# Four graph-attention layers on one core: the order of turns on five queues, a repeated cycle against a list written in full

## The chip, the core and the metric

One Trainium2 chip, of which the kernel uses one core. The metric is the device time of one execution in microseconds (us): the median of the runs, from the first instruction to the last and what lies around them. Before the change it is 2925.74 us (3 runs, 2920.73 to 2927.1).

## What is computed

The input is 32 graphs (batches) of 512 nodes with 256 features each, and one 512 x 512 adjacency matrix for all. Four pre-normalised graph-attention layers follow each other, and each adds its result to x:

```python
h = jnp.maximum(_layernorm(x, axis=-1), 0.0)
x = x + _L0_gnn_ref(h, adj, ...)   # 4 heads of 64, masked softmax over neighbours, elu
h = jnp.maximum(_layernorm(x, axis=-1), 0.0)
x = x + _L1_gnn_ref(h, adj, ...)   # mlp 256->512, full attention (no mask), mlp 512->256, masked attention
h = jnp.maximum(_layernorm(x, axis=-1), 0.0)
x = x + _L2_gnn_ref(h, adj, ...)   # masked attention with self edges, elu
h = jnp.maximum(_layernorm(x, axis=-1), 0.0)
x = x + _L3_gnn_ref(h, adj, ...)   # masked attention, relu
```

In each attention e[i,j] = leaky_relu(s_i + t_j), the softmax runs over j, and the result is attention @ (h @ W). The batches do not depend on each other.

## The kernel before

Each batch is a chain of about 100 pieces of matrix work (TensorE, PE), with 150 pieces on VectorE (DVE), 136 on ScalarE (ACT), 4 on GpSimd (POOL) and 2 on SyncE (SP) between them. Five Python generators write them (`tensor_batch`, `vector_batch`, `scalar_batch`, `pool_batch`, `sync_batch`), and every `yield` ends one piece, a *turn*. Before each instruction stand the semaphore waits for what it reads and for the buffer it overwrites. Every queue runs in the order in which its instructions were written.

Three batches are in flight at a time, in three *lanes* (batch modulo 3). A lane has its own R, Z, hT, hw and rowt tiles, whose names end in the lane's number, and its own ring of PSUM banks: banks 0 to 2, banks 3 to 5, and for lane 2 banks 6 and 7 alone (`RINGS`). The tiles O1, oT, HA and junk exist once, so that only one batch at a time can be in the wide part of layer 1.

What sets the order of the turns is the table `TURNS` with the function `in_turns`: for each queue a string for the beginning, a *cycle* that is repeated for every batch, and a string for the end. A digit d in the cycle means: one turn of batch t - d. A `w` is a turn of the weight loading (splitting the weights into a high and a low part, turning the masks).

The names used below, with the lines of the profile:

- PE: L515 all three-part matmuls (`mm3`: high x high, high x low, low x high); L536 transposes of the normalised rows; L560 the transpose TM of the column maxima tm; L572 the transpose "row" of the exponentials E; L584 attention of the layers 1b, 2 and 3 (`attend`); L620 attention of layer 0, one group of 64 instructions for each head; L672 the transposes zT of the tile Z after the full attention; L698 transposes of the residual. The matmuls with `wm2` are the second mlp, 24 of them, and those with `hsr` form S, the column sums.
- DVE: L916 adds zT to O1; L920 and L924 make the low part oTlo; L793 makes the attention weights P in the tile R (four for each row); L846, L848 and L854 give a head's output y0; L857 and L859 add it to x; L767 gives tm; L771 to L777 give A; L930 the low part of the second mlp's output; L806 and L808 hsr; L745 and L742 the variance ve.
- ACT: L1168 makes the high part oThi from O1; L1068 copies projected rows out of PSUM; L1031 and L1022 are the pairs "sx, sq" (`entry_sums`), sum and squares of the x that has been loaded for the batch three later; L1175 and L1177 take the second mlp's output out of PSUM, two of each; L1077 gives E; L1102 and L1104 are a head's exponential and relu; L1083 scales hw; L1045 normalises.
- POOL: L1248 raises ve to the power -1/2 (`power`), with L1250 or L1252 and L1254; L499 makes low parts of weights (`gpsimd_lo`).

In order of the batch, the place that the text speaks of most is this: four zT transposes, each followed by L916 on DVE and L1168 on ACT and a low part on DVE; then 24 `wm2` matmuls in four groups of six, of which each waits for its low part; the last group ends the result in two banks, three matmuls for each. L1175 and L1177 take the two banks out, L930 and L806/L808 follow, and S on PE waits for hsr.

Of the kernel before, what the change touches and what calls it, by code (L numbers as in the profile page):

```python
# [13 lines left out]
B, N, F = 32, 512, 256  # L14
# [52 lines left out]

TURNS = {
    "pe": (
        ("wwww00ww0000000w0ww0ww1ww0www00w1w0111w1ww100ww00001w10000100000011100000000000000120000000012000000"  # L70
         "0000000010101121122121211020211000101020110000001101121111112111020120011010011111020111111100010010"
         "0111111"),
        ("1120011101001010112200112212212021122220221111111121101122110021122121211112021121111122212122111111"),
        ("4453344434333443443553445545545354455555355444444444443455344553544545444445354444444555455454544433"
         "4442233323223232334242334443434243344444433233433333332342433442433434333334243333333444434344333322"
         "3331122212112121223131223233323132323333312222222232211223232132233223322223132223222233323232232211"
         "2220011110001010112020112212212021122220221111211111110122110022110112122110010000111200001111001020"
         "1002212000000000000001111000100000122000000000200010000121111100100001111010110000000111100111000010"
         "01010001011111000"),
    ),  # L80
    "dve": (
        ("wwwwwwwww0000w000000w00w0w000w01w00000w0w000000w00w1000000w1w100w11001101010w01011001000110100000000"
         "010w010100010001100000w00000000000001011111000111101011100002000001000100200001110100212121110202122"
         "2222010220002101111011011001120012120110101112121121112101010111111121112212002201110220002122122001"
         "02011100100"),
        ("2222221122200222111221220110101122010000010202100022221111211121112122102221121101100110110211012211"
         "11111111110100000222111220022001012002021211122122"),
        ("5555554455355534545544553434334344554333435335333554554444534544445545545344455443344443343554454344"
         "4434344444444345353544433555534345333534445455455543434444444244243334434423232333244322222224423322"
         "4434433343333343434244344334223332332323324433432333332233333333224424333424244223232244233344344344"  # L90
         "2332333333313133332222331221212232311112131131132333212222223222313321233232323211122212122221233222"
         "3222212222121211313322231133113121213132223323332312222122222022022121112201010001110221001020021002"
         "2221111211111212210220122111201001110110012112201101101100011020110000001111002110100000200001120202"
         "2100000000000010000000010000100000100000100101101110110011121110201200000120000000000000010202211002"
         "1111001100101011101001000000111001011000110000111011111110000000"),
    ),
    "act": (
        ("wwwwwww0000w00www0w000wwww0wwwwwwww11w11w10ww0w100wwwww1w1w1w1w0000w00w1w20w000020020000000000010000"
         "0000000200000010200001000100000200001111000100100001010021120002012100002110010000111000101010101100"
         "2011010101110010011101021111001011000010011020110101211101101101022202"),  # L100
        ("2022021001220022121122012202220011222120122122112212212221121112211222102211112222112112111110212211"
         "122222211202112121012111211122100002"),
        ("5355353434553355454545345555353344555345455455445545545545454544355554454445445555454544344454545454"
         "5545455445355544443444545445433343545332224424442424343342434424442233444423344343444334344443343334"
         "4344443423334433434334432333433434434343444334244333323343433334422324242312133131331133322333223311"
         "3311223332312332322333333233222222333232233323122233332222323222212333232323333223312322122323222231"
         "2131213312102202002202220121211220222000122210211221221122122222111121122212201212111221212112210111"
         "1102211022211002000011020001100021120212211000100121000000100010000000000001200101011100111100101001"
         "0201110000111101000020020010000000011110000100121001100000110011111010000110110011000011001011011001"
         "010100010110001001111000"),  # L110
    ),
    "pool": (
        ("wwwwwwww0wwwwwwwww10w0w20"),
        ("2202"),
        ("5553444233132201010120"),
    ),
    "sp": (
        ("0"),
        ("32"),
        ("2165544313200"),  # L120
    ),
}
FIRST, ENDS = 3, 4


def in_turns(batch, turns, loading):
    going, loads = {}, loading()

    def go(b):
        if 0 <= b < B:  # L130
            if b not in going:
                going[b] = batch(b)
            next(going[b], None)
# [12 lines left out]
    for left in [loads] + list(going.values()):
        for _ in left:
            pass

# [1199 lines left out]
```

## Time and profile before

| | |
|---|---|
| median of 3 runs | 2925.74 us (2920.73 to 2927.1) |
| the profiled execution | span 2924.5 us from first to last instruction; its own time is not listed apart from the runs', the span is 1.2 us under the median |
| PE busy | 2864.4 us, 98% of the span, 25624 matmuls |
| PE weight loads (PEld) | 2637.4 us, 90% |
| DVE, ACT, POOL busy | 2449.0 us (84%), 2306.6 us (79%), 209.0 us (7%) |
| DMA | 42.06 MB; 2 to 4% of the 16 engines outside the first microseconds |
| granted TensorE clock | mean 0.995 of full speed |

How to read it: "busy" is the union of an engine's instructions. A matmul's end is modelled and overlaps the start of the next, so that PE looks busy up to some 0.15 us after it ran out of work; the distance from start to start tells more. "Idle before" is the engine's idle time ahead of an instruction, "<-" names what ended it. The chain of work is followed back from the last instruction, at each step to what released it.

### The profile page before, as it was taken

Reading aid. Unit: us, or ns where it says so; the run is one execution under the profiler, and the core shown is the slowest. Engines: PE = TensorE matmul, PEld = TensorE weight load, DVE = VectorE, ACT = ScalarE, POOL = GpSimd, SP = SyncE. Lnnn points to the kernel's source line nnn. Section 1 sums busy time; section 2 is a strip of 40 time slices with the busy share of each in tenths; the row PEclk is TensorE's granted clock in tenths of the full one; section 3 lists DMA queues with packets and bytes.
Section 4 is the critical chain, followed back from the end, with each engine's and each line's share of the span. In section 5 each row is a group of like instructions: output and inputs, shape, how many; then the busy total and the mean of one; then the engine's idle time right before and its main releaser. Section 6 shows DMA issues by size and latency. Waiting matters only on the chain.

```text
span 2924.5 us, 66977 instructions
## 1 busy us (share of the span) xinstructions
PE 2864.4 (98%) x25624; PEld 2637.4 (90%) x25624; DVE 2449.0 (84%) x7049; ACT 2306.6 (79%) x6303; POOL 209.0 (7%) x410
## 2 busy tenths in 40 slices
PE   7999999999999999999999999999999999999998
PEld 7899999899999999999999999999999999999886
DVE  6788888888888888888888888888888888888866
ACT  6678778778778787788787788787787877887776
POOL 2000000000000000000000000000000000000000
PEclk9999999999999999999999999999999999999999
DMA  2000000000000000000000000000000000000000
GB/s 80 1 11 14 16 16 16 16 1 16 16 16 16 16 1 16 16 16 16 2 16 16 16 16 16 2 16 16 16 16 13 5 16 16 16 15 2 2 1 30
DMA packets 16799, 42.06 MB, mean 14 GB/s; under 512 B 5344, under 2 KB 7392, under 8 KB 16480
## 3 DMA queue, kind: packets, MB, share of 16 engines
q1 hardware_dynamic: 16480, 37.77, 3.7%
q8 instruction: 205, 3.36, 0.5%
q14 instruction: 114, 0.93, 0.1%
HBM read 20.99 MB, written 16.78 MB: 13 GB/s over the span
## 4 chain that ended last, share of the span: by engine, by line
PE 85%; ACT 9%; DVE 4%; issue 1%; POOL 0%; DMA 0%
PE bank L515 45%; PE bank L584 23%; PE bank L620 7%; PE bank L536 4%; PE bank L572 3%; ACT junk L1022 3%; ACT junk L1031 2%; PE bank L672 1%; DVE O L916 1%; ACT Z L1175 1%; PE bank L560 1%; PE bank L698 1%; ACT Z L1068 1%; DVE oTlo L920 1%; ACT hT2hi L1177 0%
## 5 line engine op out<-in xcount | busy, mean ns | idle before, releaser
L584 PE MATMUL bank<-hw,R 128*128 128x257 f32 x3072 | 707.8, 381 | 1.6 <-ACT hw L1083 1.0
L584 PEld LDWEIGHTS bank<-hw,R 128*128 128x128 f32 x3072 | 567.0, 191 | 74.7 <-issue 3.6
L793 DVE SCALAR_TENSOR_TENSOR R<-bank,E,mask_ne 128x512 f32<-128x512 f32 x640 | 448.9, 741 | 3.1 <-PE bank L572 0.7
L1248 POOL TENSOR_TENSOR rs<-ve,mhalf 128x4 f32<-128x4 f32 x128 | 140.6, 1099 | 2659.4 <-DVE ve L745 1655.8
L1045 ACT ACTIVATE Z<-x,nm,rs 128x256 f32<-128x256 f32 x512 | 276.6, 595 | 52.7 <-DVE x L1010 32.0
L515 PE MATMUL bank<-wfc_hi,oThi 128*128 128x256 f32 (+1 forms) x1024 | 303.3, 296 | 0.0
L515 PE MATMUL bank<-wfc_hi,oTlo 128*128 128x256 f32 (+1 forms) x1024 | 289.8, 283 | 0.0
L515 PE MATMUL bank<-wfc_lo,oThi 128*128 128x256 f32 (+1 forms) x1024 | 289.7, 283 | 0.0
L620 PE MATMUL bank<-hw,R 128*64 128x65 f32 x8192 | 268.3, 224 | 0.3 <-DVE R L793 0.3
L620 PEld LDWEIGHTS bank<-hw,R 128*64 128x64 f32 x8192 | 250.3, 138 | 20.1 <-issue 9.9
L1068 ACT COPY Z<-bank 128x258 f32<-128x258 f32 (+1 forms) x512 | 180.9, 371 | 42.6 <-PE bank L515 41.9
L515 PEld LDWEIGHTS bank<-wfc_hi,oThi 128*128 128x128 f32 x1024 | 193.7, 189 | 4.9 <-DVE hT2lo L815 1.7
L515 PEld LDWEIGHTS bank<-wfc_lo,oThi 128*128 128x128 f32 x1024 | 194.6, 190 | 0.0
L515 PEld LDWEIGHTS bank<-wfc_hi,oTlo 128*128 128x128 f32 x1024 | 194.5, 190 | 0.0
L1077 ACT ACTIVATE E<-A,kshift 128x4 f32<-128x4 f32 (+1 forms) x352 | 83.6, 289 | 127.4 <-DVE A L777 127.3
L1083 ACT ACTIVATE hw<-Z,hw 128x256 f32<-128x256 f32 x384 | 179.8, 503 | 1.2
L1022 ACT ACTIVATE Z<-x,sx 128x256 f32<-128x256 f32 x256 | 129.0, 505 | 44.9 <-DVE x L984 44.6
L515 PE MATMUL bank<-HAhi,oThi 128*128 128x258 f32 x512 | 161.8, 316 | 2.1 <-DVE oTlo L886 2.1
L572 PE MATMUL bank<-identr,E 128*128 128x128 f32 x1024 | 152.8, 276 | 10.4 <-ACT E L1077 10.4
L515 PE MATMUL bank<-HAlo,oThi 128*128 128x258 f32 x512 | 145.4, 284 | 0.0
L515 PE MATMUL bank<-HAhi,oTlo 128*128 128x258 f32 x512 | 144.8, 283 | 0.0
L536 PE MATMUL bank<-identr,Z 128*128 128x128 f32 x1024 | 139.3, 276 | 2.8 <-ACT Z L1045 2.6
(262 smaller groups left out, 8351.0 us busy)
## 6 DMA issues: line engine op xcount, KB each, us to landing
x<-in_x_dram SPq DMA_DIRECT2D x32, 512.0 KB, 3.5
out_dram<-x SPq DMA_DIRECT2D x31, 512.0 KB, 2.6
R<-in_adj_dram SPq DMA_DIRECT2D x2, 512.0 KB, 5.6
Z<-in_L_gnn_mlp_w_dram SPq DMA_DIRECT2D x2, 512.0 KB, 5.4
O<-in_L_gnn_W_fc_dram SPq DMA_DIRECT2D x1, 1024.0 KB, 6.9
out_dram<-x SPq DMA_DIRECT2D x4, 128.0 KB, 2.4
R<-in_L_gnn_W_dram SPq DMA_DIRECT2D x1, 256.0 KB, 3.9
R<-in_L_gnn_W_hand_dram SPq DMA_DIRECT2D x1, 256.0 KB, 6.5
```

Of the source, the lines that this page charges most:

```text
L515: i = e.matmul(out, u, v, start=first and q == 0, stop=last and q == 2, skip_group_check=not group)
L536: i = e.transpose(bk[:, n * 128:(n + 1) * 128], hn[:, n, k * 128:(k + 1) * 128], ident[:, :])
L572: i = e.transpose(bk[:, n * 128:(n + 1) * 128], m["E"][:, 0, h, n:n + 1].broadcast_to([128, 128]), ident[:, :])
L584: ins = e.matmul(bk[:, 0:257], P[:, j, i * 128:(i + 1) * 128], hw[:, j, 0:257], start=(j == 0), stop=(j == NBLK - 1))
L620: ins = e.matmul(bk[c:c + 64, i * 66:i * 66 + 65], P[:, (4 * h + j) % PTILES, i * 128 + c:i * 128 + c + 64], hv[:, j, h, 0:65], start=(j = ...
L793: e.scalar_tensor_tensor(P[:, t, :], bank_of(b, "row", p)[:, :], m["E"][:, 1, h, j:j + 1], mask[:, j, :], ALU.max, ALU.mult).then_inc(up(" ...
L1022: e.activation(hns[b % LANES][:, n, :] if l else junk[:, n, :], xs[b % XSLOTS][:, n, :], ACT.Square, bias=m["sx"][:, n:n + 1], scale=-floa ...
L1045: e.activation(hn[:, n, :], x[:, n, :], ACT.Relu, bias=m["nm"][:, n:n + 1], scale=m["rs"][:, n:n + 1]).then_inc(up("hn", b))
L1068: e.copy(raw[s][:, i, 0:n], bank_of(b, f"h{l}", i)[:, 0:n]).then_inc(up("raw", b))
L1077: e.activation(out, m["A"][:, src, 0:nh, :], ACT.Exp, bias=shift[:, 0:1], scale=sc).then_inc(up("E", b))
L1083: e.activation(hw[:, n, 0:256], raw[s][:, n, 0:256], ACT.Copy, scale=hw[:, n, 256:257]).then_inc(up("hw", b))
L1248: e.tensor_tensor(m["rs"][:, :], m["ve"][:, :], mhalf[:, :], ALU.pow).then_inc(up("rs", b))
```

## The change

Only the order of the turns is another. `TURNS` now holds for each queue one string of all its turns, in which a digit or letter is the batch in base 36 (0 to v); `in_turns` reads it one by one. No instruction is added or removed, and each queue has as many turns as before (PE 3224, DVE 4825, ACT 4394, POOL 147, SP 64). Line numbers below the table are 57 higher than before.

```diff
@@ TURNS @@
     "pe": (
-        ("wwww00ww0000000w0ww0ww1ww0www00w1w0111w1ww100ww00001w10000100000011100000000000000120000000012000000"
...
-        ("1120011101001010112200112212212021122220221111111211101121122110021122121112021121111122212122111111"),
...
+        "w00www0000ww0w0000ww0ww11ww0ww0ww1ww1110ww1ww11w00100001100001100200200122002000000000000200010120000111000100"
...
     "pool": (
-        ("wwwwwwww0wwwwwwwww10w0w20"),
-        ("2202"),
-        ("5553444233132201010120"),
+        "wwwwwwwwwwwwwwwwwww0100021113222433354446555766687779888a999baaacbbbdcccedddfeeegfffhgggihhhjiiikjjjlkkkmlllnm"
+        "mmonnnpoooqppprqqqsrrrtsssutttvuuvuvv"
...
@@ in_turns @@
-    going, loads = {}, loading()
-
-    def go(b):
-        if 0 <= b < B:
-            if b not in going:
-                going[b] = batch(b)
-            next(going[b], None)
-
-    start, cycle, end = turns
-    for c in start:
-        if c == "w":
-            next(loads, None)
-        else:
-            go(int(c))
-    for t in range(FIRST, B - ENDS):
-        for c in cycle:
-            go(t - int(c))
-    for c in end:
-        go(B - 1 - int(c))
-    for left in [loads] + list(going.values()):
+    going, loads = [batch(b) for b in range(B)], loading()
+    for c in turns:
+        next(loads if c == "w" else going[int(c, 36)], None)
+    for left in [loads, *going]:
         for _ in left:
             pass
```

In the middle of the new strings (batches 6 to 21) the order repeats every three batches, where before it repeated every batch. Three places, as the built programs have them:

**ACT at batch 11's second mlp, before.** From the last three L1168 of batch 11 (tile O1) to its first L1175; Z1, x1 are tiles of batch 10's lane, Z2 of batch 11's.

```order
L1168 CAST oThi<-O1 128x512 x3
L1068 COPY Z1<-bank3 128x258
L1068 COPY Z1<-bank4 128x258
L1031 ACTIVATE junk,sx1<-x1 128x256
L1022 ACTIVATE junk,sq1<-x1,sx1 128x256
...
L1175 ACTIVATE Z2<-bank6,b2 128x512
L1177 ACTIVATE hT2hi,hs2<-Z2 128x512
```

The same place after the change (line numbers 57 higher); Z0 is batch 12's head:

```order
L1225 CAST oThi<-O1 128x512 x2
L1125 COPY Z1<-bank3 128x258
L1125 COPY Z1<-bank4 128x258
L1088 ACTIVATE junk,sx1<-x1 128x256
L1079 ACTIVATE junk,sq1<-x1,sx1 128x256
L1225 CAST oThi<-O1 128x512
...
L1225 CAST oThi<-O1 128x512
...
L1159 ACTIVATE Z0<-Z0 128x256
L1161 ACTIVATE Z0<-Z0 128x256
L1232 ACTIVATE Z2<-bank6,b2 128x512
L1234 ACTIVATE hT2hi,hs2<-Z2 128x512
```

Before, all four pairs (L1031, L1022) stand between the last L1168 and L1175. After it, one pair stands ahead of the last L1168 but one, one more ahead of the last, and two behind; batch 12's head pair (L1102 and L1104, now L1159 and L1161) stands ahead of L1175 and no longer behind it.

**DVE at the same place, before.** From the last L916 of batch 11 to batch 10's tm; R0, D0, Z0 are batch 12's.

```order
L916 TENSOR_TENSOR O1<-bank7,O1 128x512
L920 TENSOR_TENSOR oTlo<-O1,oThi 128x512
L857 SCALAR_TENSOR_TENSOR Z0<-Z0 128x256
L859 SCALAR_TENSOR_TENSOR x0<-Z0,x0 128x4x64
L924 TENSOR_TENSOR oTlo<-O1,oThi 128x512
L793 SCALAR_TENSOR_TENSOR R0<-bank2,E0,mask_ne 128x512 x4
L846 TENSOR_SCALAR D0<-bank0 128x4
L848 RECIPROCAL rD0<-D0 128x4
L854 TENSOR_TENSOR Z0<-bank0,rD0 128x256
L745 TENSOR_SCALAR ve1<-sq1 128x4
L767 TENSOR_REDUCE tm1<-Z1 128x1
```

And after the change:

```order
L973 TENSOR_TENSOR O1<-bank7,O1 128x512
L977 TENSOR_TENSOR oTlo<-O1,oThi 128x512
L850 SCALAR_TENSOR_TENSOR R0<-bank2,E0,mask_ne 128x512
L981 TENSOR_TENSOR oTlo<-O1,oThi 128x512
L850 SCALAR_TENSOR_TENSOR R0<-bank2,E0,mask_ne 128x512 x2
L903 TENSOR_SCALAR D0<-bank0 128x4
L905 RECIPROCAL rD0<-D0 128x4
L911 TENSOR_TENSOR Z0<-bank0,rD0 128x256
L802 TENSOR_SCALAR ve1<-sq1 128x4
L824 TENSOR_REDUCE tm1<-Z1 128x1
```

Three P (one of them ahead of the last low part) stand where four stood behind it, and L857, L859 have gone behind tm. On PE the head's group L620 of batch 12 that stood ahead of the zT now stands between the last zT and the `wm2` matmuls.

**POOL at the beginning, before.**

```order
L499 TENSOR_TENSOR wfc_lo<-O,wfc_hi 128x512 x4
L1248 TENSOR_TENSOR rs<-ve,mhalf 128x4
L1250 TENSOR_SCALAR nm<-mv 128x4
L1254 TENSOR_TENSOR nm<-nm,rs 128x4
L1248 TENSOR_TENSOR rs<-ve,mhalf 128x4
L1252 TENSOR_SCALAR nm<-sx 128x4
L1254 TENSOR_TENSOR nm<-nm,rs 128x4
L499 TENSOR_TENSOR wm_lo<-Z,wm_hi 128x256 x4
L499 TENSOR_TENSOR wha_lo<-R,wha_hi 128x256 x2
L499 TENSOR_TENSOR w_lo<-rowt,w_hi 128x256 x2
```

And after the change:

```order
L556 TENSOR_TENSOR wfc_lo<-O,wfc_hi 128x512 x4
L1305 TENSOR_TENSOR rs<-ve,mhalf 128x4
L1309 TENSOR_SCALAR nm<-sx 128x4
L1311 TENSOR_TENSOR nm<-nm,rs 128x4
L556 TENSOR_TENSOR wm_lo<-Z,wm_hi 128x256 x4
L556 TENSOR_TENSOR wha_lo<-R,wha_hi 128x256 x2
L556 TENSOR_TENSOR w_lo<-rowt,w_hi 128x256 x2
L556 TENSOR_TENSOR w_lo<-x,w_hi 128x256 x2
L1305 TENSOR_TENSOR rs<-ve,mhalf 128x4
L1307 TENSOR_SCALAR nm<-mv 128x4
```

The group with L1250 is batch 0's second normalisation, the one with L1252 batch 2's first. Batch 2's and all low parts of weights now stand ahead of batch 0's.

## Rows read from the trace of the kernel before

**Rows 1.** The page's first part: busy time, share of the span, instructions.
```profile
PE 2864.4 (98%) x25624; PEld 2637.4 (90%) x25624; DVE 2449.0 (84%) x7049; ACT 2306.6 (79%) x6303; POOL 209.0 (7%) x410
```

**Rows 2.** Windows: start:end, length, busy us (x), PEclk, DMA share, GB/s.
```profile
1010.58:1277.07 266.49, 264.39 (x2389) 244.19 (x2388) 227.72 (x658) 214.32 (x589) 18.06 (x37) 1.00 0.04 13
```

**Rows 3.** Timeline of POOL: start, us, instruction [idle before <-releaser].
```profile
1010.58 1.20 POOL L1248 TENSOR_TENSOR rs<-ve,mhalf 128x4 f32<-128x4 f32 x1 [32.41 <-DVE ve L742]
...
1277.07 1.20 POOL L1248 TENSOR_TENSOR rs<-ve,mhalf 128x4 f32<-128x4 f32 x1 [32.39 <-DVE ve L742]
```

**Rows 4.** The chain of waits, 1060 to 1150 us: start, us, what.
```profile
1060.01 1.73 PE bank L584 x8
1061.75 2.87 PE bank L515 x24
1064.61 2.02 PE bank L620 x64
1066.63 3.07 PE bank L515 x24
...
1076.87 0.88 PE bank L672 x8
...
1079.16 0.45 PE bank L672 x4
...
1079.63 0.69 DVE O L916
...
1082.73 0.42 ACT junk L1031 x2
...
1086.87 0.58 ACT Z L1175
...
1090.58 0.97 PE bank L515 x6
```

**Rows 5.** Who waited for whom, whole span: us in total, times, longest.
```profile
PE bank L560 <- DVE tm L767: 14.6, 33, 1.4
PE bank L572 <- ACT E L1077: 10.4, 30, 1.2
...
PEld bank L515 <- DVE hsr L808: 11.8, 28, 2.6
```

**Rows 6.** Timeline of all engines at the same place.
```profile
1083.44 2.72 DVE L793 SCALAR_TENSOR_TENSOR R<-bank,E,mask_ne 128x512 f32<-128x512 f32 x4
...
1085.20 0.39 PE L515 MATMUL bank<-oThi,wm_lo 128*128 128x512 f32 x1
...
1085.88 0.39 PE L515 MATMUL bank<-oThi,wm_lo 128*128 128x512 f32 x1
...
1086.78 0.67 ACT L1175 ACTIVATE Z<-bank,b 128x512 f32<-128x512 f32 x1
...
1086.98 0.15 DVE L767 TENSOR_REDUCE tm<-Z 128x1 f32<-128x4 f32 x1
...
1087.28 0.29 PE L560 MATMUL bank<-identr,tm 128*128 128x128 f32 x1 [0.33 <-DVE tm L767]
...
1090.00 0.40 ACT L1102 ACTIVATE Z<-Z 128x256 f32<-128x256 f32 x1
```

**Rows 7.** Groups of instructions, whole span: ... xcount | busy us, mean ns | idle before.
```profile
L1168 ACT CAST oThi<-O 128x512 fp32r<-128x512 f32 x128 | 79.4, 622 | 51.9 <-DVE O L916 51.9
```

**Rows 8.** Timeline of POOL at the beginning.
```profile
58.08 1.04 POOL L1248 TENSOR_TENSOR rs<-ve,mhalf 128x4 f32<-128x4 f32 x1 [23.44 <-DVE ve L742]
...
59.57 1.03 POOL L1248 TENSOR_TENSOR rs<-ve,mhalf 128x4 f32<-128x4 f32 x1
```

**Rows 9.** Windows at the beginning and the end, columns as in rows 2.
```profile
70.00:140.00 70.00, 65.19 (x637) 58.87 (x637) 56.78 (x152) 44.06 (x108) 1.45 (x3) 0.98 0.01 1
...
2790.00:2855.40 65.40, 61.67 (x401) 56.47 (x401) 46.59 (x145) 46.60 (x124) 1.63 (x3) 0.97 0.00 1
2855.40:2920.30 64.90, 54.66 (x281) 46.35 (x279) 39.94 (x134) 41.57 (x119) 4.37 (x9) 0.89 0.04 16
```

More of the change, by code:

```diff
@@ new lines @@
+        "00102101001000001122112110020000111011110110001000011112200201110000111110011001111100101002211111113322223332"
+        "32322113322111123123121211111122222222322223112232212211112222131221221222112121132222232244333344443343322443"
+        "32222332423342222232333333323333332244222233233433332423333333222322322443333333554444554545454335544333344353"
+        "44533333443444444344445334433333544454444435344444443334334335544444446655565666556554465564444564554654444445"
+        "55555554556554455644455445565555464554554555445454455665555577666677776667655776655556657566755555655666666666"
@@ new lines @@
+        "67556665575566656766665756665666655565655776666666887777887878787668877666677686778666667767777776777786677666"
+        "87776678777768677767777666767667887777779988898999889887798897777897887987777778888888878898877889777887788988"
+        "887978878878887787877889988888aa9999aaaa999a988aa998888998a899a888889889999999999a8899988a8899989a99998a899989"
+        "99988898988aa9999999bbaaaabbabababa99bbaa9999aa9b9aab99999aa9aaaaaa9aaaab99aa999baaa99abaaaa9b9aaa9aaaa999a9a9"
+        "9abbaaaaaaccbbbcbcccbbcbbaacbbcaaaabcabbacbaaaaaabbbbbbbbabbcbbaabbcaaabbaabbcbbbbacabbabbabbbaababaabbccbbbbb"
@@ new lines @@
+        "ddccccddddcccdcbbddccbbbbccbdbccdbbbbbcbbccccccccccdbbcccbbdbbcccbcdccccbdbcccbccccbbbcbcbbddccccccceeddddeede"
+        "dededcceeddccccddcecddecccccddcddddddcddddeccddcccedddccdeddddcecdddcddddcccdcdccdeeddddddffeeefefffeefeeddfee"
+        "fddddefdeedfeddddddeeeeeeeedeefeeddeefdddeeddeefeeeedfdeedeedeeeddededdeeffeeeeeggffffggggfffgfeeggffeeeeffege"
+        "ffgeeeeefeeffffffffffgeefffeegeefffefgffffegefffeffffeeefefeeggfffffffhhgggghhghghghgffhhggffffggfhfgghfffffgg"
+        "fggggggfgggghffggfffhgggffghggggfhfgggfggggfffgfgffghhggggggiihhhihiiihhihhggihhigggghighhgihgggggghhhhhhhhghh"
@@ new lines @@
+        "ihhgghhiggghhgghhihhhhgighhghhghhhgghghgghhiihhhhhjjiiiijjjjiiijihhjjiihhhhiihjhiijhhhhhihhiiiiiiiiiijhhiiihhj"
+        "hhiiihijiiiihjhiiihiiiihhhihihhjjiiiiiiikkjjjjkkjkjkjkjiikkjjiiiijjikijjkiiiiijjijjjjjjijjjjkiijjiiikjjjiijkjj"
+        "jjikijjjijjjjiiijijiijkkjjjjjjllkkklklllkklkkjjlkkljjjjkljkkjlkjjjjjjkkkkkkkkjkklkkjjkkljjjkkjjkklkkkkjljkkjkk"
+        "jkkkjjkjkjjkkllkkkkkmmllllmmmmlllmlkkmmllkkkkllkmkllmkkkkklkkllllllllllmkklllkkmkklllklmllllkmklllkllllkkklklk"
+        "kmmlllllllnnmmmmnnmnmnmnmllnnmmllllmmlnlmmnlllllmmlmmmmmmlmmmmnllmmlllnmmmllmnmmmmlnlmmmlmmmmlllmlmllmnnmmmmmm"
@@ L80 @@
+        "strrssstrrrrsssrtsssssrtrsssssssrrsrrrsrssssrttssuusttttuuutututtssuuttsssstuststtsssssstutttttttsttuuttssttus"
+        "ttssttssttttusttsttstttssststssttttuutttvvuuvuuvvuvuvuuttvvuuttttuutvtuuvtttttuttuuuuuuuuuuvuttuuvvtttuuuvuuuu"
+        "uttuuutvvuuvtvvvuutvvvvttutvvuvvuvvuuuutvvvvvvvvvvvvvvuuvvvtvvvvvtvvvvvvvvuvuvvvvvvvuuuuuuuuuvvuuvvvvuvuvvvvvv"
+        "vvuuuuuuvvuuvvvuvvuuvuuuvuvuvvvvvv"
     ),
     "dve": (
[L82 to L85, printed above, removed]
@@ L111 @@
+        "stssttsusssuuuttsssstutsstssssttstsusssttttttsststtsssststttsssstttssttttttustststsstssssttusttstutstststttttt"
+        "ssuuuussutuvtvtvvttttvttvututtuutvtttvvvuuttttvuuttuttttuuutttttuuuuututtttvttutuuuuuuttttuuvttuuuuuuutttvuuuu"
+        "vuuttttttvvvvuuvvuuuttvtvvvuuttvvvvuvuuvvuuvtvvvvvvutvuvvuvvvvuvvvvuvvvvvuuuvvuvvuuuvvuuuttvuvvvvvuvuuuvvvvvuu"
+        "vvvvvvvvvuuvuvvuvvvvuuuuvvvvuvvuuvvuvvvvvvvuuuuvuvvvvuuuuvuuvvuvvvvuuvvuuuuuuvuvuvuuvuvvvvvvvvvvuuuuvvvv"
     ),
     "pool": (
-        ("wwwwwwww0wwwwwwwww10w0w20"),
```

123 lines of the change are left out of this document (87 added, 36 removed).

## The prediction, made before the changed kernel ran

> **What bounds the kernel now.** I read the page's first part, then windows, then the chain of waits, then who waits for whom. PE is busy 98% of the span, DVE 84%, ACT 79% [rows 1]. The order cannot remove PE work, so the question is how much of the span is not PE work. In the middle three batches take 1277.07 - 1010.58 = 266.5 us, 88.8 us each [rows 3], and PE counts as busy 264.4 us of these [rows 2]. A matmul's end is modelled, so I add up a batch by distances from start to start: narrow L515 2.87/24 = 0.120 us, L584 1.73/8 = 0.217, L620 2.02/64 = 0.032, transposes 0.88/8 = 0.110 [rows 4], wide L515 (1085.88 - 1085.20)/3 = 0.227 [rows 6]. The code has for a batch 300 narrow, 96 L584, 256 L620, 96 transposes and 48 wide: 36.0 + 20.8 + 8.2 + 10.6 + 10.9 = 86.5 us. So **2.3 us a batch** are something else, at most 65 us over 28 batches. 0.8 us of it no order takes away, the restart behind each of the four L620 groups: 24 L515 take 3.07 us behind one, 2.87 otherwise [rows 4]. About 1.5 us are left, and most of that stands at one place.
>
> The chain shows the place: it leaves PE at 1079.61, behind the third group of zT, and comes back at 1090.58, at S [rows 4]. Between them lie L916, four pairs of L1031 and L1022 (1082.73 to 1086.87), two L1175 with L1177, and hsr. PE waits there three times: TM for tm, the row for E, S for hsr. The whole span shows 14.6 us for 33 such TM, 10.4 us for 30 such rows, and 28 waits of the weight load for hsr [rows 5]: once in each batch of the middle. In one number: from the last matmul of the second mlp's first bank (1085.88) to S (1090.58) are 4.70 us [rows 4, 6]; PE's work in them is 0.23 + 3 x 0.227 + 0.11 (TM) + 2.02 + 0.20 (L620) + 0.44 (row) = 3.68. **Lost: 1.02 us a batch.**
>
> **The change, part by part.**
>
> *ACT at this place.* L1175 starts at 1086.78 although its bank was ready at 1085.88 + 0.39 = 1086.27 [rows 6]: ACT was in the last pair. Before, all four pairs (4.1 us) stand behind the last L1168. After, two do, with the head pair L1102, L1104. Counted from the end of the third zT: L916 0.69, two L1168 of 0.62 [rows 7] with one pair (4.14/4 = 1.03) between, two pairs (2.07), the head pair 0.8 (L1102 is 0.40 [rows 6]), together 5.8 us. PE comes to the end of the first bank after a zT group 0.44, the moved L620 2.2 and 21 wide matmuls 4.8, together 7.4. So ACT no longer sets when L1175 starts: it starts at about 1086.30 and all behind it 0.48 us earlier.
>
> *DVE at this place.* tm stands at 1086.98 because of four L793 (2.72 us) behind the last low part [rows 6]. Two stand there now, 1.36 us less, and PE has an L620 group more (2.2 us) in front of the second mlp. TM's wait, 0.33 us by the profile [rows 6], goes. That alone gives nothing: row and S, which wait for the chain over L1175, are late next. What counts is S.
>
> *What stays.* From L1175's start to S are 1090.58 - 1086.78 = 3.80 us [rows 4, 6], the same instructions as before. From 1085.88 that is 0.42 + 3.80 = 4.22 against 3.68 of PE work: 0.54 us stay lost. Gain: 1.02 - 0.54 = **0.48 us a batch, 28 times: 13.4 us.** Bounds: nothing (ACT or DVE late for another reason), and 1.02 x 28 = 28.6 us.
>
> *Lane 2.* It has two banks, and every third batch is longer: the order now differs from lane to lane, which it could not before. I see moves both ways there (four L1083 stand ahead of the copies that free its banks, the heads' pairs behind them), and take nothing; bounds -5 to +10 us of gain, that is a third or so of a microsecond for each of 28 batches.
>
> *Beginning.* POOL waits 23.44 us for batch 0's variance, and batch 2's first normalisation stands behind it (59.57) [rows 8]. Now it stands ahead, with the ten low parts of weights, so POOL's idle time takes them. Batch 2 can then enter PE some 16 us of PE work earlier, and fill what batches 0 and 1 leave: 70.0 - 65.2 = 4.8 us between 70 and 140 us [rows 9]. I take 2 us of gain; bounds 5 of gain, 3 of loss (ten L499 ahead of batch 0's second normalisation).
>
> *End.* Behind batch 29's last attention (it ends at 2855.4) only batches 30 and 31 are left. I counted the matmuls behind it: 109 narrow, 64 attention steps of two L584 and 44 transposes before, 45.7 us of PE work; 139, 80 and 65 after, 58.6 us. In the last stretch PE idles 10.2 us in 64.9, at a granted clock of 0.89; in the stretch ahead of it 3.7 in 65.4 at 0.97 [rows 9]. 13 us of work go from the second kind to the first: 13 x (19/46 - 4/62), where 19 is 64.9 less 45.7, is some 4.5; part of it comes back where three batches now share. I take **3 us of loss**; bounds 0 and 7.
>
> *Queues else.* SP issues loads and stores in the order it had. POOL in the middle does the entering batch's power first; it stands idle for 32 us before [rows 3], so this costs nothing, and its cover is that idle time.
>
> **Sum**: 2925.7 - 13.4 - 2 + 3 = **2913 us**. The profiled span lies 1.2 us under the median, so the sum may be made on either.
>
> **A rule against this bound.** PE's weight loads are busy 2637.4 us, 90% [rows 1]. The Trainium skill (Perfetto Trace Analysis, Identifying the Most-Contended Engine) says that busy matmuls are a bad measure of headroom and that the busy share of the weight loads is one of the two good ones. By it 10% of the span, 287 us, would be open to a better order. The distances from start to start, 86.5 us of 88.8, speak against it here: loads of this kernel are shorter than the matmuls that cover them.
>
> **The rivals.**
>
> - *No change.* The 0.48 us turn up again elsewhere: the chain from L1175 on is untouched, and the new order has places with less between a matmul and what waits for it, the first matmuls of the full attention among them. Against it: those places show no wait now. Time 2920 to 2931, say 2925.
> - *Slower: the head pair ahead of L1175.* It waits for L854, which stands behind three L793 and the last low part. From the third zT, with 0.69 for an L916 or a low part [rows 4] and 2.72/4 = 0.68 for an L793 [rows 6]: two L916 and two low parts 2.8, L793 0.7, the last low part 0.7, two L793 1.4, y0 0.8 (from the last L793's end, 1086.16, to tm at 1086.98), the pair 0.8: 7.2 us, and PE's first bank is ready after 7.4. Only 0.2 us covers it. Every tenth by which DVE comes later than that goes into S; from 0.7 late on the gain is gone. At 1.0 late the loss at the place is 0.54 + 0.8 = 1.34 us, 0.32 more than now, x28 = 9 us, with 1 us for the ends: 2936 us. For it: DVE is busy 84% [rows 1] and has little reserve. Against: 0.69 is an instruction's whole length, and the next can start before its end; 7.2 is the long end.
> - *Larger gain.* Chains begin early enough that all of 1.02 us goes, or lane 2 gives its bounds too: 2925.7 - 28.6 + 1 = 2898 us.
> - *The room of the weight loads.* If an order could fill half of PEld's idle time by packing loads, 143 us would go: 2782 us.
> - That the change does not do what it says is out: the lists of instructions are the same, turn for turn.
>
> **Chances.** Forecast 0.54 (2903 to 2919), larger gain 0.13, weight loads 0.01, no change 0.18, slower 0.14. A measurement of this kernel can tell 0.2%, 5.9 us, from no change; so faster 0.54 + 0.13 + 0.01 = 0.68, same 0.18, slower 0.14. The range reaches from 2898, the larger gain's point, over no change to 2931; outside stay half of the larger gain and most of slower, 0.19.
>
> **What would show it.** Right: no wait of TM for tm in the middle; the chain stays on PE between zT and the second mlp, leaves it at L1175 only, and the four pairs L1031, L1022 are gone from it; S 4.2 us behind the first bank's last matmul; three batches in 265 us instead of 266.5; PE idle at the end 2 to 4 us more. Wrong: a wait for the head pair or for L854 ahead of L1175, a new wait in the full attention, or a pitch of 266 us or more. If the pitch falls as said and the time does not, the end is at fault.

## The result, and the profile after

The changed kernel takes 2908.0 us (median of 4 runs, 2904.9 to 2908.4), the kernel before 2924.7 beside it: ratio 0.9938, 95% interval [0.9924, 0.9952]. So it is faster, by 17 us; the forecast was 2913, so the gain is 4 to 5 us larger than forecast. The profiled execution took 2907.97 us, its span is 2906.2 us.

The page's first part, as [rows 1]:

```profile
PE 2847.7 (98%) x25624; PEld 2630.2 (91%) x25624; DVE 2448.4 (84%) x7049; ACT 2333.5 (80%) x6303; POOL 216.1 (7%) x410
```

No engine has less to do; PE's busy time falls by 17 us because it holds waits too. Windows at the beginning and the end, as [rows 9], and of three batches, as [rows 2]:

```profile
70.00:140.00 70.00, 68.38 (x667) 63.83 (x668) 53.02 (x134) 44.16 (x106) 1.45 (x3) 0.96 0.03 9
140.00:210.00 70.00, 65.38 (x656) 60.51 (x654) 59.31 (x170) 56.34 (x158) 4.84 (x9) 1.00 0.01 2
...
1008.92:1273.09 264.17, 262.77 (x2389) 243.33 (x2389) 227.64 (x657) 217.12 (x589) 18.95 (x37) 1.00 0.04 13
...
2688.30:2821.60 133.30, 131.55 (x1097) 121.88 (x1096) 107.08 (x308) 100.70 (x257) 4.78 (x9) 1.00 0.01 5
2821.60:2901.90 80.30, 67.02 (x363) 55.97 (x363) 50.67 (x171) 55.69 (x158) 5.89 (x12) 0.96 0.04 16
```

The last two windows are the stretch between the last attentions of batches 28 and 29, and what lies behind it up to PE's last instruction. Three batches take 264.2 us instead of 266.5 [rows 3], 0.77 us a batch less. The profile's waits, as [rows 5] (L617 is L560 of before, L629 and L572 are L572 and L515):

```profile
PE bank L629 <- ACT E L1134: 18.8, 31, 2.3
...
PEld bank L572 <- DVE hsr L865: 17.2, 31, 2.8
...
PE bank L617 <- DVE tm L824: 3.3, 3, 1.4
```

Of TM's 33 waits 3 are left, 11.3 us less. But the row's wait has grown by 8.4 us and that of the weight load for hsr by 5.4: the same chain is waited for one piece later, as the forecast had it. The chain of waits no longer runs through this stretch, so the place is read from the timeline of all engines, at the same batch as [rows 6]:

```profile
1079.69 0.60 ACT L1225 CAST oThi<-O 128x512 fp32r<-128x512 f32 x1
...
1081.25 0.60 ACT L1225 CAST oThi<-O 128x512 fp32r<-128x512 f32 x1
...
1084.21 0.42 DVE L911 TENSOR_TENSOR Z<-bank,rD 128x256 f32<-128x256 f32 x1
...
1084.62 0.15 DVE L824 TENSOR_REDUCE tm<-Z 128x1 f32<-128x4 f32 x1
1084.67 0.42 ACT L1159 ACTIVATE Z<-Z 128x256 f32<-128x256 f32 x1 [0.74 <-DVE Z L911]
...
1085.27 0.39 PE L572 MATMUL bank<-oThi,wm_lo 128*128 128x512 f32 x1
...
1085.69 0.69 ACT L1232 ACTIVATE Z<-bank,b 128x512 f32<-128x512 f32 x1 [0.16 <-PE bank L572]
...
1086.17 0.27 PE L617 MATMUL bank<-identr,tm 128*128 128x128 f32 x1
...
1088.80 0.62 PE L629 MATMUL bank<-identr,E 128*128 128x128 f32 x4 [0.34 <-ACT E L1134]
...
1089.52 0.38 PE L572 MATMUL bank<-wha_hi,hsr 128*128 128x256 f32 x1
```

ACT now stands idle for PE ahead of L1232, where it had been inside its last pair. The head pair waits 0.74 us for y0 (L1159 for L911). The forecast had named such a wait as a sign of being wrong, but it ends early enough here: it costs nothing. L1232 starts 0.42 us behind the first bank's last matmul (forecast 0.42), S 4.25 us behind it (forecast 4.22, before 4.70). **0.45 us a batch, forecast 0.48.** Counted from the first `wm2` matmul, S gains 0.33 (8.93 us instead of 9.26): the first bank is ready 0.11 us later, as an L677 group now stands directly ahead.

The other 0.32 us I had not foreseen. Distances from start to start, added up turn by turn over batches 6 to 20, put most of it into layer 1's `wfc` projections: the first of the four turns is 0.11 us shorter, the second 0.11, the third 0.06, and the fourth 0.07 longer, 0.21 in sum. The first in the trace of before:

```profile
1208.43 0.69 DVE L872 TENSOR_TENSOR oTlo<-O,oThi 128x512 fp32r<-128x512 f32 x1 [0.19 <-ACT oThi L1120]
...
1209.03 0.28 PE L515 MATMUL bank<-wfc_hi,oTlo 128*128 128x258 f32 x1
...
1209.18 0.39 PE L515 MATMUL bank<-wfc_hi,oThi 128*128 128x258 f32 x1
...
1209.40 0.28 PE L515 MATMUL bank<-wfc_lo,oThi 128*128 128x258 f32 x1
```

From 1209.03 to 1209.40 are 0.37 us for two matmuls that take 0.24 elsewhere: the fourth low part was ready at 1209.12, when PE wanted it. No row of waits names it. After the change the matmuls at this place follow each other in 0.12 us. Only this first turn waits for low parts. The second ends before a TM of the next batch and the third begins behind one; after the change that TM stands ahead of the fourth, so their part is in part only moved. The other turns differ by up to 0.2 us both ways. No experiment tests the `wfc` part by itself.

### The profile page after: what moved, and what is told of

Read it like the earlier page. It is cut to its first block and busy times, and to the rows that moved or that the text cites. A ratio compares the mean times of both kernels' runs of the same rounds, so it can differ in the third digit from the quotient of the medians.

```text
span 2906.2 us, 66977 instructions
## 1 busy us (share of the span) xinstructions
PE 2847.7 (98%) x25624; PEld 2630.2 (91%) x25624; DVE 2448.4 (84%) x7049; ACT 2333.5 (80%) x6303; POOL 216.1 (7%) x410
## 5 line engine op out<-in xcount | busy, mean ns | idle before, releaser
L641 PEld LDWEIGHTS bank<-hw,R 128*128 128x128 f32 x3072 | 563.5, 190 | 81.4 <-issue 10.4
L850 DVE SCALAR_TENSOR_TENSOR R<-bank,E,mask_ne 128x512 f32<-128x512 f32 x640 | 448.3, 743 | 12.9 <-PE bank L677 6.5
L1305 POOL TENSOR_TENSOR rs<-ve,mhalf 128x4 f32<-128x4 f32 x128 | 133.9, 1046 | 2630.8 <-DVE ve L802 2260.0
L572 PE MATMUL bank<-wfc_hi,oThi 128*128 128x256 f32 (+1 forms) x1024 | 302.1, 295 | 0.0
L1102 ACT ACTIVATE Z<-x,nm,rs 128x256 f32<-128x256 f32 x512 | 271.6, 593 | 23.3 <-DVE x L1067 18.1
L572 PE MATMUL bank<-wfc_hi,oTlo 128*128 128x256 f32 (+1 forms) x1024 | 289.8, 283 | 0.0
L572 PE MATMUL bank<-wfc_lo,oThi 128*128 128x256 f32 (+1 forms) x1024 | 289.7, 283 | 0.0
L677 PEld LDWEIGHTS bank<-hw,R 128*64 128x64 f32 x8192 | 254.0, 140 | 27.9 <-issue 19.1
L677 PE MATMUL bank<-hw,R 128*64 128x65 f32 x8192 | 272.1, 226 | 3.2 <-DVE R L850 3.2
L572 PEld LDWEIGHTS bank<-wfc_hi,oThi 128*128 128x128 f32 x1024 | 194.7, 190 | 0.3
L572 PEld LDWEIGHTS bank<-wfc_lo,oThi 128*128 128x128 f32 x1024 | 194.2, 190 | 0.1
L572 PEld LDWEIGHTS bank<-wfc_hi,oTlo 128*128 128x128 f32 x1024 | 194.3, 190 | 0.0
L1140 ACT ACTIVATE hw<-Z,hw 128x256 f32<-128x256 f32 x384 | 169.8, 499 | 2.3
L629 PE MATMUL bank<-identr,E 128*128 128x128 f32 x1024 | 151.3, 276 | 19.4 <-ACT E L1134 18.8
L572 PE MATMUL bank<-HAhi,oThi 128*128 128x258 f32 x512 | 160.4, 313 | 0.0
L572 PE MATMUL bank<-HAlo,oThi 128*128 128x258 f32 x512 | 145.0, 283 | 0.0
L572 PE MATMUL bank<-HAhi,oTlo 128*128 128x258 f32 x512 | 144.8, 283 | 0.0
L629 PEld LDWEIGHTS bank<-identr,E 128*128 128x128 f32 x1024 | 116.1, 137 | 28.9 <-issue 22.6
```

Of the source, the lines that this page charges most:

```text
L572: i = e.matmul(out, u, v, start=first and q == 0, stop=last and q == 2, skip_group_check=not group)
L629: i = e.transpose(bk[:, n * 128:(n + 1) * 128], m["E"][:, 0, h, n:n + 1].broadcast_to([128, 128]), ident[:, :])
L641: ins = e.matmul(bk[:, 0:257], P[:, j, i * 128:(i + 1) * 128], hw[:, j, 0:257], start=(j == 0), stop=(j == NBLK - 1))
L677: ins = e.matmul(bk[c:c + 64, i * 66:i * 66 + 65], P[:, (4 * h + j) % PTILES, i * 128 + c:i * 128 + c + 64], hv[:, j, h, 0:65], start=(j = ...
L850: e.scalar_tensor_tensor(P[:, t, :], bank_of(b, "row", p)[:, :], m["E"][:, 1, h, j:j + 1], mask[:, j, :], ALU.max, ALU.mult).then_inc(up(" ...
L1102: e.activation(hn[:, n, :], x[:, n, :], ACT.Relu, bias=m["nm"][:, n:n + 1], scale=m["rs"][:, n:n + 1]).then_inc(up("hn", b))
```

## The experiments

A turn is written (batch, number). "The changed kernel's place" is the second mlp with what stands beside it on all three engines.

### The two ends

In the trace, the end of batch 2 comes at 392.4 us before and at 397.6 after, 5.2 later; from batch 28's end to the last instruction 4.1 us are gained. I had forecast 2 us of gain and 3 of loss: in the traces both signs are wrong and the sum is right. Three kernels take one part each.

```diff
 start_of_before: every queue of TURNS
-  new order
+  order of before up to PE's turn (1, 99) and all that it waits for; then the new order
```


> The changed kernel, with the beginning in the old order: on each queue the turns up to batch 1's last matmul are those of before, the rest is in the new order. Theory A (the new beginning loses: batches 0 to 2 leave PE 5 us later than before, the middle and the end gain): about 5 us under the changed kernel, 2903 us, ratio to before 0.992. Rival B (the late beginning is how the new middle gets ahead, it pays back later): as the changed kernel or slower, 0.994 or more.

```diff
 start_of_after: every queue
-  order of before up to PE's turn (1, 99) and all that it waits for
+  new order up to there; then the order of before
```


> The kernel before, with the beginning in the new order up to batch 1's last matmul, the rest in the old order. Theory A: about 5 us slower than before, 2930 us, ratio 1.002. Rival B: same as before, 1.000 or less.

```diff
 end_of_after: every queue
-  order of before, from PE's turn (28, 15) on
+  new order from there on
```


> The kernel before up to batch 28's PE turn 15, and from there the new order on all queues. Theory C (the end gains by itself some 4 us, as the difference of the two traces says, where I had forecast a loss of 3): 2920 us, ratio 0.9985. Rival D (the end is better only because of the state in which the new middle leaves it): same or slower, 1.000 to 1.002.

Measured: start_of_before 2906.15 us, ratio 0.9938 [0.9924, 0.9951], which is 1.9 us under the changed kernel and the same ratio; start_of_after 2926.7, ratio 1.0005 [0.9995, 1.0014]; end_of_after 2923.6, ratio 0.9988 [0.9979, 0.9997].

Theory A, 5 us for the beginning, falls. By start_of_after the new beginning costs between -1.5 and 4 us, so it may cost nothing. The 5.2 us of the changed kernel's trace are not a property of its order: that is taken up below.

Theory C holds for the end, and Rival D falls: end_of_after gains 3.5 us by its ratio, between 1 and 6. But 1.9 us of its trace's gain lie between the ends of batches 26 and 28 (175.9 us instead of 177.8), and these the forecast counts with the middle. From batch 28's end to the last instruction, three traces with the old end take 219.0 to 222.0 us, and ten with the new end, searched left out, 217.9 to 220.2. So the 4.1 us of the two traces above are the high end; the means lie 1.4 us apart.

GpSimd's order alone was the forecast's reason for the beginning:

```diff
 pool_of_before: TURNS["pool"]
-  new order
+  order of before; the other four queues as changed
```


> The changed kernel with GpSimd's whole queue in the order of before: batch 0's second normalisation ahead of batch 2's first and of the last low parts of weights. Forecast's step: batch 2's earlier entry gained 2 us, so 2910. Theory D: the beginning's loss that the trace shows (5.4 us at the end of batch 1) comes from batch 0 waiting for the normalisation that was put behind ten low parts, so 2903 to 2905. Rival E: it comes from the order on PE, GpSimd's order is worth nothing: 2908.

2909.4 us (2908.9 to 2910.4), ratio 0.9950 [0.9935, 0.9965]. Theory D falls: the old order gives nothing back. All four runs lie above the changed kernel's four (2904.9 to 2908.4), by 1.4 us in the median, but the intervals overlap, so the times don't decide between the forecast's 2 us and Rival E, which gives this order no worth. The trace does show what the new order is good for. PE's wait ahead of batch 1's first rows, in this kernel and in group_early (below), which has the changed kernel's order there:

```profile
69.36 1.94 PE L629 MATMUL bank<-identr,E 128*128 128x128 f32 x8 [10.40 <-ACT E L1134]
```
```profile
64.21 1.94 PE L629 MATMUL bank<-identr,E 128*128 128x128 f32 x8 [3.21 <-ACT E L1134]
```

On ACT's queue batch 2's first L1102 stands ahead of this E. ACT is idle 8.49 us there, until GpSimd has done batch 2's first normalisation (63.4 us) and the low parts `wm_lo` (66.1). Both stand behind batch 0's second normalisation in the old order, as the forecast said. Batch 2 ends at 399.2 us in this trace, and at 392.4 to 394.3 in three of the changed order.

### The place at the second mlp

First the place was put into the kernel of before, on PE, ACT and DVE at once, batches 4 to 25:

```diff
 place_all: PE
- L620 (13, second last group), hsr's L515 (11), zT, zT, hT's L515 x2, zT, L515, zT, L515, wm2
+ hsr's L515 (11), hT's L515 x2, zT, zT, zT, L515, zT, L620 (13), L515, wm2
```

The lines are those of batch 12, the numbers in brackets are batches, and L515 stands for a turn of projections. ACT and DVE have their part of it too: two pairs ahead of the last L1168, the head pair ahead of L1175, L793 between the low parts. It is not the changed kernel's place to the turn: one L515 is left between the L620 group and `wm2`, and L857 and L859 (now L914 and L916) stand among the low parts instead of behind tm.

> The kernel before, changed only at the second mlp of batches 4 to 25, as the changed kernel has it: on PE the head's group (turn 13 of the next batch) behind the last zT, and the projections in front of the zT; on ACT two L1168 between the pairs and the head pair ahead of L1175; on DVE two L793 earlier. Theory E (the gain of the middle at this place is 0.45 us a batch, because L1175 no longer waits behind the pairs): 22 x 0.45 = 10 us under before, ratio 0.9966. Rival F (the gain of 0.75 us a batch of the middle comes from the rest of the order, and the wait returns elsewhere if only this place is changed): 1.000.

3004.3 us, ratio 1.0273 [1.0259, 1.0287]. All theories fall: it is 80 us slower, 3.6 us a batch. Its waits:

```profile
PE bank L629 <- ACT E L1134: 33.0, 30, 1.3
PE bank L617 <- DVE tm L824: 21.2, 33, 1.4
PE bank L572 <- DVE hsr L865: 14.7, 23, 1.8
```

Half of the loss is here: from the first `wm2` matmul to S are 11.08 us, where there were 9.26 before and 8.93 after the change. The other half stands ahead of the place. There PE waits 0.5 to 0.6 us for the hsr of the batch before (batches 10 to 12), where before the change it did not wait: the L620 group that was moved had been the cover for it. Further waits for the copies and for zT stand behind it. This kernel does not say what the place is worth, since it is neither an exact copy nor has the neighbours for it. So from here on one thing is undone in the changed kernel. The orders differ from lane to lane, and the lines shown are those of batch 13: in its lane three pairs stand ahead of the last L1225 and all four L850 ahead of L981, more than at batch 11.

```diff
 pairs_late: ACT, batches 4 to 27 (p is a pair L1088, L1079)
- L1125 x2, p, L1225, p, p, L1225, p, L1159, L1161, L1232
+ L1125 x2, L1225, L1225, p, p, p, p, L1159, L1161, L1232
```


> The changed kernel (2908.0 us), in which ScalarE's four pairs of L1088 and L1079 are put back where they stood before, behind the last L1225 and ahead of L1232, for batches 4 to 27. Theory A, the step of the prediction with the moved head's group of L677 as what gives the room: from the third zT 0.69 + 2 x 0.62 + 4.14 + 0.8 for the head pair = 6.9 us of ScalarE against 7.4 of PE, so L1232 is still not late: 2906 to 2911. Rival B, the pairs' place itself is what gained: 24 x 0.45 = 11 us are lost, 2919.

```diff
 group_early: PE, batches 4 to 27
+ L677 (next batch, second last group)
  zT, zT, zT, L572 x12, zT
- L677
  wm2
```


> The changed kernel, in which PE's second last group of L677 of the next batch's layer 0 goes back ahead of the four zT (in batches 4 to 27), everything else as changed. Theory A: the 2.2 us of PE work between the zT and the second mlp are what keeps ScalarE and VectorE off S's path; from the third zT they then need 5.8 us and PE 5.2, the wait at S is as before the change or 0.1 us longer, 24 x 0.45 to 24 x 0.6: 2919 to 2923. Rival B, the group's place is worth nothing since the pairs are spread: 2908. Rival C, the low parts also come late for the second mlp: above 2930.

```diff
 weights_late: DVE, batches 4 to 27
- L850, L977, L973, L977, L973, L977, L850 x3, L981, L903, L905, L911
+ L977, L973, L977, L973, L977, L981, L850 x4, L903, L905, L911
```


> The changed kernel, in which all L850 of the head stand behind the last low part of the second mlp again, as before the change (batches 4 to 27), the rest as changed. Theory A (the prediction's: TM's wait costs nothing of its own): 2906 to 2910, with TM's wait back or not. Rival B: what VectorE had in front of it in this place is part of the 0.78 us per batch, 0.2 to 0.3 us a batch come back: 2913 to 2915.

| | us | ratio | loss a batch |
|---|---|---|---|
| pairs_late | 2916.5 | 0.9973 [0.9962, 0.9984] | 0.35 |
| group_early | 2943.7 | 1.0065 [1.0048, 1.0082] | 1.49 |
| weights_late | 2936.9 | 1.0042 [1.0027, 1.0057] | 1.20 |

(The loss is against the changed kernel's median, over 24 batches; by the ratios to before it is 0.43, 1.55 and 1.27.) pairs_late lies between Theory A and Rival B, nearer to B. group_early lies in Rival C's range, above 2930, and its trace bears C out: PE waits for L981's low parts 7 times, 4.1 us in all, which the changed kernel never does. For weights_late both theories fall. The timelines say how. From the first `wm2` matmul of batch 13, in us:

| | L911 (y0) ends | L1232 starts | S starts |
|---|---|---|---|
| before | 5.57 | 5.46 | 9.26 |
| after | 3.89 | 5.10 | 8.93 |
| pairs_late | 3.89 | 5.43 | 9.24 |
| group_early | 5.61 | 6.42 | 10.23 |
| weights_late | 6.34 | 7.14 | 10.95 |
| place_all | 6.47 | 7.27 | 11.08 |

**S starts 3.80 to 3.83 us behind L1232 in all six.** What sets L1232 differs. In the last three it starts 0.80 us behind y0: the head pair stands ahead of it and waits for y0. That is the mechanism of the forecast's rival on the slower side, and weights_late shows it, where only DVE's order was touched. Batch 11 in its timeline (the chain from y0 over the pair and L1232 to S):

```profile
1088.65 0.42 DVE L911 TENSOR_TENSOR Z<-bank,rD 128x256 f32<-128x256 f32 x1
...
1089.56 0.42 ACT L1161 ACTIVATE Z<-Z 128x256 f32<-128x256 f32 x1
...
1089.88 0.67 ACT L1232 ACTIVATE Z<-bank,b 128x512 f32<-128x512 f32 x1
...
1093.69 0.39 PE L572 MATMUL bank<-wha_hi,hsr 128*128 128x256 f32 x1
```

In the changed kernel L1232 could start at 3.89 + 0.80 = 4.69, and the bank is there at 5.10: 0.41 us to spare in the lanes of batches 12 and 13, and 0.26 in batch 11's (y0 at 4.04), where the forecast had 0.2. DVE's four weights behind the last low part take these and make L1232 1 to 2 us late, by the lane; batch 13 is the worst. In my expectation I had looked at TM's wait alone and forgotten y0, which stands behind the same weights. TM's wait is not what costs: weights_late shows 9.5 us of it in 10 waits, and the loss is 29 us.

In pairs_late ACT is late by itself. I had counted 6.9 us from the third zT for what took longer, since each L1225 waits for its L973, and DVE makes a low part between two of them. The last L1225 ends at 0.62, four pairs at 4.77, the head pair at 5.52; L1232 comes 0.33 us late and S 0.31. So the pairs' place and PE's moved group are both needed; each of them was given the whole gain in one of my theories.

### The beginning and the granted clock

The beginnings of pairs_late, group_early and weights_late have the changed kernel's order up to batch 3, and yet their batch 2 ends at 393.9, 394.3 and 392.4 us, not at 397.6. Windows 30 to 60 and 60 to 90 us, of the changed kernel, and of weights_late:

```profile
30.00:60.00 30.00, 26.91 (x367) 25.04 (x366) 24.50 (x52) 18.43 (x50) 11.36 (x15) 0.83 0.01 1
60.00:90.00 30.00, 27.09 (x253) 24.67 (x253) 24.76 (x64) 15.83 (x37) 6.64 (x11) 0.77 0.06 19
```
```profile
30.00:60.00 30.00, 25.76 (x388) 24.27 (x388) 27.01 (x62) 20.73 (x57) 14.89 (x20) 0.94 0.01 2
60.00:90.00 30.00, 27.13 (x314) 25.14 (x315) 25.72 (x66) 13.87 (x35) 2.13 (x5) 0.83 0.06 19
```

The granted clock makes most of the difference. A mean of 0.83 over 30 us is 10 us at 1.2 GHz and 20 at 2.4; 0.94 is 3.6 us. From 0 to 140 us the changed kernel's trace has 24 us at half clock (mean 0.91). These three, start_of_after, and of the old beginning before, start_of_before and end_of_after have 14 (0.95), and place_all, with the old beginning, 3 (0.99). Batch 2 ends so:

| half clock in 0 to 140 us | new beginning | old beginning |
|---|---|---|
| 3 us | | 389.6 |
| 14 us | 392.4, 393.9, 394.1, 394.3 | 392.4, 392.6, 393.6 |
| 24 us | 397.6 | |

So 10 us more at half clock stand for 3 to 4 us of delay, and at the same clock the two beginnings are 0.8 us apart in the mean, inside their scatter. Against weights_late another 1 us of the 5.2 had been lost ahead of the first group of L677 (33.65 against 32.70).

In all five traces of the new beginning PE stands idle 2.85 us for R ahead of this group, and the clock falls at 33 to 35 us. It falls again at 60 to 63 us, in four of the five inside an idle stretch of 3.2 us ahead of batch 1's rows. So I filled these gaps with matmuls that nobody reads:

```diff
 warm_start: tensor_batch
-                    warm(bk, 6)
+                    warm(bk, 17)
...
             for k in range(2):
+                    if l == 1 and k == 0:
+                        warm(bk, 20)
```


> The changed kernel with 31 more matmuls on batch 0's tiles that nobody reads, where PE waits for batch 0 alone at the beginning: 11 more in front of its first group of L677 (2.9 us idle) and 20 in front of its layer 1 (5.7 us idle). The order of the turns is untouched. Theory G, the granted clock is what the two ends turn on (0.91 in 0 to 60 and in 60 to 140 us is 25 us at 1.2 GHz, half of which is lost PE work): with the idle gaps filled the clock in 0 to 140 rises to 0.97 or more, and the time falls to 2900 to 2904. Rival H, the clock varies from execution to execution whatever PE does: 2906 to 2909. Rival I, the added matmuls stand in the way of batches 1 and 2: above 2910.

2909.3 us, ratio 0.9942 [0.9928, 0.9955]. By the time alone Theory G falls. Its timeline tells the two additions apart:

```profile
62.03 1.94 PE L631 MATMUL bank<-identr,E 128*128 128x128 f32 x8 [3.22 <-ACT E L1136]
63.77 1.71 PE L418 MATMUL bank<-x,rowt 128*128 128x2 f32 x8
65.33 7.26 PE L583 MATMUL bank<-hT0hi,w_hi 128*128 128x512 f32 x20
72.43 1.04 PE L595 MATMUL bank<-identr,Z 128*128 128x128 f32 x8
```

Up to here PE was 5.3 us ahead of the changed kernel's trace (0.9 of it already ahead of the first addition), with the clock at 1.00 throughout 30 to 60 us. Then the 20 stood behind an idle stretch, not in it, and ran for the most part at half clock (0.52 granted between 60 and 70 us): 0.36 us each, where the 11 take 0.24. Two pieces on, PE is 1.3 us behind that trace: 6.6 us lost, of which some come back later. Batch 2 ends at 398.4. The last run keeps the 11 alone:

```diff
 warm_first: tensor_batch
-                    warm(bk, 6)
+                    warm(bk, 17)
```


> The changed kernel with only the first 11 of the added matmuls, in front of batch 0's first group of L677. In the run with both additions the 11 had brought PE's turn 7 of batch 1 to 5.3 us earlier than in the changed kernel's trace, at a granted clock of 1.00 in 30 to 60 us, and the 20 behind them ran at half clock from 65.3 to 72.4 us and took 6.6 us away again. Theory G, the clock in 30 to 60 us decides when the lanes fill: the end of batch 2 comes 4 to 6 us earlier than in the changed kernel's trace (397.6), 392 to 394, and the time is 2902 to 2905. Rival H: the changed kernel's own executions already reach the better clock mostly, the trace was the worse one: the end of batch 2 at 392 to 394 all the same, the time 2906 to 2908. Rival M: something else takes up the gain before batch 2, its end at 397 or later, the time 2908 or more.

**2903.0 us (2902.4 to 2904.3, 5 runs), ratio 0.9916 [0.9902, 0.9930]**: 5 us under the changed kernel in the median, with intervals that overlap, and the fastest version of this study. Its timeline, the changed kernel's first, and windows:

```profile
29.17 1.63 PE L583 MATMUL bank<-hT0hi,w_hi 128*128 128x512 f32 x6
33.65 3.11 PE L677 MATMUL bank<-hw,R 128*64 128x65 f32 x64 [2.85 <-DVE R L850]
```
```profile
29.20 4.12 PE L583 MATMUL bank<-hT0hi,w_hi 128*128 128x512 f32 x17
33.72 2.66 PE L677 MATMUL bank<-hw,R 128*64 128x65 f32 x64 [0.39 <-DVE R L850]
```
```profile
30.00:60.00 30.00, 28.40 (x394) 25.77 (x392) 26.67 (x60) 20.20 (x56) 14.30 (x19) 0.94 0.01 2
60.00:90.00 30.00, 26.79 (x310) 24.59 (x309) 25.33 (x63) 14.84 (x35) 3.76 (x7) 0.83 0.06 19
```

L677 starts no earlier, but runs its 64 instructions in 2.66 us and not 3.11, and the clock does not fall there: 1.00 from 30 to 45 us in both filled kernels, 0.77 to 0.89 in the five traces without the filling. It falls later (0.94 over 30 to 60 us), and batch 2 ends at 394.6 us (expected 392 to 394). The three unfilled traces above were earlier. Beside group_early, whose first L677 starts at the same time, warm_first is 0.3 us behind all the way to batch 2's end. So the traces show 3 us of gain against the changed kernel's own trace and none against the unfilled ones with 14 us at half clock, and Rival H had a point. The filled kernel's five runs end at 2904.3 us, the changed kernel's four begin at 2904.9. That the added matmuls make the better beginning certain fits this, but is not shown.

### An order worked out further

```diff
 searched: every queue
-  new order
+  new order with single turns moved further, at all places
```


> The changed kernel with single turns moved further, at all places: each move was kept if the end came earlier when all waits were worked through with the durations of the trace of before. By this bookkeeping 8.5 us come from the beginning, 0.13 us from each batch of the middle and 4 us from the end. Theory J, the time is made of such waits alone: 15 us less than the changed kernel, 2893. Rival K, the middle's moves are worth hundredths of a microsecond that real durations spread over, and the beginning's gain goes to the clock: 2900 to 2908. Rival L, a wait whose true duration is longer than the row's median gives a loss in every batch: above 2912.

```diff
 searched_start: every queue
-  new order up to PE's turn (2, 99) and all that it waits for
+  the order of searched up to there; then the new order
```


> Of the order of the run before this one in the list, only the beginning, up to batch 2's last attention; the rest as in the changed kernel. Theory J: 8 us less than the changed kernel, 2900. Rival K: 2904 to 2908. Set beside the run with all moves it tells the beginning's part from the middle's and the end's.

searched took 2907.0 us, ratio 0.9937 [0.9923, 0.9951]. searched_start took 2903.4 to 2914.3 us in five executions, median 2908.5, ratio 0.9947 [0.9928, 0.9966]; a sixth took 5751.7 us, which stays unexplained and is left out here. Theory J falls and Rival K holds for searched. searched_start lies at the edge of K's range, too scattered to set the beginning's part beside the rest. In the middle the durations of rows had promised 0.13 us a batch. The trace of searched shows 0.11 of loss instead (from batch 2's end to batch 26's it takes 2.7 us more than the changed kernel).

## Why the prediction was right, point by point

- **ACT at this place, and what stays**: right. ACT does not set L1232, which starts 0.42 us behind the bank; S follows it in 3.83 us (forecast 3.80) and gains 0.45 us a batch of 0.48. But ACT's 5.8 us from the third zT were short. They leave out that L1225 waits for L973 with low parts between; pairs_late showed that ACT was nearer to the edge than I thought: with all four pairs behind the last L1225, L1232 came 0.33 us late where I had counted 0.5 us to spare.
- **DVE at this place**: TM's wait goes and comes back as the row's, right. "That alone gives nothing" is true of the wait, not of the move: y0 stands behind the same weights, and from there hangs the head pair. weights_late puts 1.2 us a batch on it.
- **Lane 2, taken at nothing, with all else in the middle**: mis-sized. 0.32 us a batch came, 9 us over 28 batches, 0.21 of it from the `wfc` turns in every lane. The search of the 2.3 us that are not PE work stopped at the waits that rows name. A wait of 0.1 us inside a matmul's modelled end has no row. Of the 2.3 us, 1.5 are left.
- **Beginning, 2 us of gain**: not there. More work between 70 and 140 us did come, 68.4 us of PE instead of 65.2 [rows 9]. It was paid back behind: 65.4 us between 140 and 210, where the kernel before has 69.6. The step on GpSimd was right: with its old order PE waits 10.4 us instead of 3.2, and in that trace batch 2 ends 5 to 7 us later. What failed is taking this for the whole beginning, as if nothing else in the new order cost anything there. start_of_after and start_of_before show 0 to 2 us of loss, neither clear of zero. What takes up GpSimd's part stays open.
- **End, 3 us of loss**: failed in sign; 1 to 4 us of gain. The work behind batch 29's last attention did grow by 13 us, and up to PE's last instruction 80.3 us hold the 58.6 of PE work: 21.7 lost instead of 19, 2.6 more, where the forecast had 5.4 more (13 x 19/46). What failed is the stretch ahead. Between the ends of batches 28 and 29 I took the 13 us out at the old rate of loss, 4 in 62. In fact it went from 152.9 to 133.3 us, 19.6 less for 13 us of work moved, so 6.6 us of loss went and not 0.8. It is 133.3 in nine of the ten traces with the new end, and 151.7 to 153.1 in the three with the old. A part of the 4.1 is the clock, 0.97 against 0.94 in the last 140 us.
- The sum: 13.4 and nothing for lane 2 stood for 19.5 us between the ends of batches 2 and 28; -2 + 3 stood for +5.2 - 4.1 in the traces. That the two ends cancelled to the same 1 us, each with the other sign, is luck. With them set aside, the forecast is right in its main step and 6 us short in the middle.
- The rivals: no change and the larger gain are out. The slower one has its mechanism and its price (0.80 us behind y0, one for one into S) and did not come about: DVE had 0.26 to 0.41 us to spare. The room of the weight loads did not show: PEld stays at 90 to 91%. The forecast's reason against it, short loads, does not hold for the narrow L515: a load of theirs takes 0.19 us in the timeline, and they follow each other in 0.12. What speaks against the room are the distances alone.

## What to carry to other kernels

Find the one instruction from which the late consumer hangs by a fixed latency (here L1232, 3.8 us ahead of S in all six orders of the table), then list everything in front of it on its own queue with what each waits for: the smallest distance is what a reorder has to spare, and it is spent one for one. Undo parts in the new order rather than carry a place into the old one, where it can lose the covers around it. And before a microsecond or two at the beginning is put down to an order, compare that stretch in other traces with the same order, with the granted clock beside it.

## What the runs showed of the hardware

- One order of the beginning had 14 us at half clock between 0 and 140 us in four traces and 24 in a fifth, and its batch 2 ended at 392.4 to 394.3 us and at 397.6.
- With filler matmuls in the idle stretch ahead of the attention (0.24 us each; idle 0.39 us left of 2.85) the clock was 1.00 from 30 to 45 us in two traces, without them 0.77 to 0.89 in five. Behind an idle stretch of 3.22 us fillers ran at half clock for the most part (0.36 us each) and cost 6.6 us of delay.
- Two matmuls took 0.37 us instead of 0.24 where the operand came as PE asked for it, without a row of waits.
